# Graph network in one kernel: row splitting spread over the opening of each dense pass, halves stored in parts, counting moved off the first pieces, and identity blocks added by GpSimd

## The reference, cut to what matters

```
h = relu(layernorm(x)); x = x + L0(h)     # sum over edges with 1/sqrt(degree) weights and a self loop, times W
h = relu(layernorm(x)); x = x + L1(h)     # sum over edges plus the node itself, times W.T
h = relu(layernorm(x)); x = x + L2(h)     # mean over in-edges and over out-edges, then a GRU cell
h = relu(layernorm(x)); x = x + L3(h)     # two attention layers with batch norm
```

## Time and profile before

| what | value |
| --- | --- |
| median of three runs | 7018.52 us |
| the profiled execution | 7031.45 us, span 7029.6 us |
| PE, DVE, ACT, POOL busy | 5391.5, 5294.7, 2121.9, 3234.8 us |
| dense passes 0, 1, 2 on PE | 941.4 to 1341.8, to 1747.2, to 2157.8 us |
| turned pass on PE | 2163.7 to 2620 us |
| gather of the attention layers | 2944 indirect DMAs issued by POOL |

### The profile page before, as it was taken

One profiled execution on the slowest core, in us unless ns is written; L12 is line 12 of the kernel. 1 busy time (PEld: TensorE's weight loads), 2 busy tenths in 40 slices (PEclk: granted clock), 3 DMA queues, 4 the chain that ended last, 5 costly groups with the idle time before them and its releaser, 6 DMA issues.

```text
span 7029.6 us, 88148 instructions
## 1 busy us (share of the span) xinstructions
PE 5391.5 (77%) x33473; PEld 4175.0 (59%) x33473; DVE 5294.7 (75%) x7140; ACT 2121.9 (30%) x3520; POOL 3234.8 (46%) x3274
## 2 busy tenths in 40 slices
PE   6999979899898887377777777774377777777773
PEld 5999968788686664255555555553255555555552
DVE  7999974786783335678888888876588888888876
ACT  3555544545465443111111111112111111111111
POOL 1222100000000000777777777773777777777763
PEclk9999999999999999689888888886688988888886
DMA  4333367687789990255455455452345545545553
GB/s 148 135 123 132 123 232 256 223 266 235 267 269 221 222 189 26 56 127 127 114 128 125 116 127 123 118 127 66 74 114 128 127 114 128 127 114 128 128 127 83
DMA packets 1103488, 1021.20 MB, mean 145 GB/s; under 512 B 467063, under 2 KB 957709, under 8 KB 1098870
## 3 DMA queue, kind: packets, MB, share of 16 engines
q1 hardware_dynamic: 998150, 790.99, 39.0%
q0 software_dynamic: 104976, 225.47, 13.7%
HBM read 569.77 MB, written 346.75 MB: 130 GB/s over the span
## 4 chain that ended last, share of the span: by engine, by line
POOL 42%; issue 14%; PE 4%; DVE 3%; ACT 0%; DMA 0%; SPq 0%; POOLq 0%; DVEq 0%; ACTq 0%
POOL arena L833 39%; POOL arena L841 2%; POOL segment_terms L814 1%; PE PS L1312 1%; PE PS L1390 1%; PE PS L1403 0%; PE PS L1308 0%; PE PS L1449 0%; POOL arena L819 0%; PE PS L1291 0%; DVE arena L2150 0%; DVE arena L2151 0%; DVE arena L2247 0%; DVE arena L2246 0%; DVE arena L2238 0%
## 5 line engine op out<-in xcount | busy, mean ns | idle before, releaser
L833 POOL DMA_INDIRECT arena<-table,arena x2944 | 2794.7, 949 | 897.2 <-issue 897.2
L2046 DVE TENSOR_TENSOR arena<-shift,PS 128x1664 bf16<-128x1664 bf16 (+1 forms) x768 | 1319.7, 1779 | 3.3
L1180 PE MATMUL PS<-count_pieces,node_halves 128*128 128x512 f32 (+1 forms) x4704 | 1085.8, 388 | 70.8 <-DVE count_pieces L1783 36.6
L1036 ACT ACTIVATE arena<-PS 128x396 f32<-128x396 f32 (+1 forms) x1078 | 525.2, 490 | 1949.5 <-PE PS L1390 1943.5
L1403 PE MATMUL PS<-X,arena 128*128 128x396 bf16 x5952 | 1037.8, 331 | 0.0
L1180 PEld LDWEIGHTS PS<-count_pieces,node_halves 128*128 128x128 f32 x4704 | 858.5, 189 | 242.2 <-issue 37.2
L1390 PE MATMUL PS<-arena 128*128 128x132 f32 x6272 | 964.2, 321 | 2.6 <-DVE arena L2032 2.6
L1390 PEld LDWEIGHTS PS<-arena 128*128 128x128 f32 x6272 | 928.3, 229 | 46.1 <-issue 2.8
L1368 PE MATMUL PS<-ident,arena 128*32 128x128 f32 x392 | 101.5, 413 | 1004.1 <-DMA arena<-table,arena 1004.1
L1119 PE MATMUL PS<-arena 128*128 128x49 bf16 x7936 | 804.1, 278 | 24.5 <-DVE arena L1621 22.5
L1403 PEld LDWEIGHTS PS<-X,arena 128*128 128x128 bf16 x5952 | 570.1, 97 | 418.5 <-issue 3.6
(11 more groups left out here) (373 smaller groups left out, 4986.6 us busy)
## 6 DMA issues: line engine op xcount, KB each, us to landing
arena<-counts SPq DMA_DIRECT2D x315, 896.0 KB, 4.8
segment_sums<-arena SPq DMA_DIRECT2D x96, 2176.0 KB, 10.7
counts<-arena SPq DMA_DIRECT2D x31, 3136.0 KB, 9.4
arena<-table,arena POOLq DMA_INDIRECT x2944
vec<-edge_rows SPq DMA_DIRECT2D x192, 64.0 KB
arena<-counts SPq DMA_DIRECT2D x21, 448.0 KB, 3.4
table<-arena SPq DMA_DIRECT2D x2, 3332.0 KB, 14.1
arena<-table SPq DMA_DIRECT2D x2, 3332.0 KB, 15.0
```

Of the source, the lines that this page charges most:

```text
L833: g_.indirect_dma_start(out=ring[n % RING][:, i, :], out_offset=None, in_=table_d[j][:, :], in_offset=bass.IndirectOffsetOnAxis(ap=other[: ...
L1036: c_.activation(out_rows[:, g:g + width, 0:SW], PS[:, 4 + m % 2, 0:width * SW].rearrange("p (t f) -> p t f", f=SW), ACT.Copy)\
L1180: last = t_.matmul(PS[:, 2 + g % 2, 0:w].rearrange("p (u r) -> p u r", r=CK), X2[:, blk, t, :], PC[:, n % 3, 0:units(g), b, :], start=(blk ...
L2046: last = v_.tensor_tensor(spots[t][:, lo:hi, :], block_at[:, t, :].unsqueeze(1).broadcast_to([P, hi - lo, P]), PS[:, 3, P + lo:P + hi].uns ...
```

## The change

ACT centres the rows of pass 0 while the counts are still built (`centred_rows`), so that at the opening of pass 0 DVE only divides and takes the remainder. In all three passes the splitting is no longer done in one go: `divide`, `high` and `low` of a group stand between the first pieces' widenings, and in passes 1 and 2 the first groups are split behind the last pieces of the pass before. The index tables of pass 0 move from pieces 1 to 16 to pieces 7 to 23. DVE takes four of the seven blocks of the half-size pieces, which ACT did alone. The first three pieces of passes 1 and 2 are counted by ACT, and of the later groups DVE counts every second piece in pass 1 and ACT the others in pass 2. SP stores `node_halves` in seven parts behind pieces 14, 26, ..., 86, and issues the first three transposed loads of the turned pass as the last three pieces are widened. POOL adds the identity to the widened counts (`add_own`, 49 additions of 128x128 in each of passes 0 and 1), and PE's identity matmuls go; a piece with such a block waits for the semaphore `own_added`. To have a semaphore for that, PE's score turning in the attention layers waits for `logits` of the batch before, which its own earlier instruction has already waited for.

```diff
+        ALONE = 3
         def by_vector(n):
-            k, m = n // SLOTS, n % SLOTS
-            return (SLOTS - NPB) * k + min(m + 1, SLOTS - NPB)
+            return n + 1
+        def counted(k, g, p, by):
+            if units(g) < 2:
+                return k == 2
+            if by == "vector":
+                return k == 1 and (p >= AHEAD if g == 0 else g < SHARE or p % 2 == 0) or k == 2 and (g > 0 or p >= AHEAD)
+            return k > 0 and g == 0 and p < AHEAD or k == 2 and g >= SHARE and p % 2 == 1
+        AHEAD = 3
...
# SP
-                    if k == 2 and m == 2:
-                        sp.wait_ge(s["parts_ready"], 3 * NMG)
-                        sp.dma_start(x2_d.rearrange("(b p) f -> p b f", p=P), X2[:, :, :, :].bitcast(f32).rearrange("p b t f -> p b (t f)"))\
-                          .then_inc(s["x2_stored"], 16)
-            sp.wait_ge(s["conv_a"], 3 * SLOTS)
-            sp.wait_ge(s["conv_v"], by_vector(3 * SLOTS - 1))
-            sp.wait_ge(s["stair_sums"], 3 * STAIR)
+                    for i in range(NMG):
+                        if k == 2 and m == 14 + 12 * i:
+                            sp.wait_ge(s["parts_ready"], 2 * NMG + i + 1)
...
+                if m < 3:
+                    sp.wait_ge(s["conv_a"], 3 * SLOTS - 2 + m)
+                    sp.wait_ge(s["conv_v"], by_vector(3 * SLOTS - 3 + m))
...
# POOL
+            def add_own(k, m):
+                n, g = piece(k, m), m // NPB
+                pool.wait_ge(s["conv_a"], n + 1)
+                pool.wait_ge(s["conv_v"], by_vector(n))
+                for j in OWN[m]:
+                    part = PC[:, n % 3, (j - 4 * g) // 2, (j - OT) % PB, j % 2 * P:(j % 2 + 1) * P]
+                    g_.tensor_tensor(part, part.bitcast(f32), ident[:, :], ALU.add).then_inc(s["own_added"], 1)
...
# ACT, while the counts are built
+                        c_.activation(centred_rows[:, j - 1, :], X[:, j - 1, :], ACT.Identity, bias=stat[:, 1, j - 1:j])\
+                          .then_inc(s["row_stats"], 1)
# ACT, last pieces of a pass
+                        if m >= SLOTS - 4:
+                            high(k + 1, m - (SLOTS - 4))
                 if k < 2:
-                    for m in range(3):
-                        conv(k + 1, m)
-                    act.wait_ge(s["piece_used"], SLOTS * (k + 1))
...
+                    conv(k + 1, 0)
+                    high(k + 1, 4)
+                    conv(k + 1, 1)
+                    high(k + 1, 5)
+                    conv(k + 1, 2)
...
# PE
+                if own and OWN[m]:
+                    pe.wait_ge(s["own_added"], own_through(n))
...
-                if p == 0 and own:
-                    lo, hi = nodes_of(g)
-                    for j in range(lo, hi):
-                        for t in range(HALF):
-                            t_.matmul(PS[:, 2 + g % 2, (j - 4 * g) * P:(j - 4 * g + 1) * P], X2[:, j - OT, t, :], identr[:, :],
-                                      start=False, stop=False)
```

More of the change, by code:

```diff
@@ L356, in piece, with widened, columns @@
             return SLOTS * k + m
+        ALONE = 3
         def by_vector(n):
-            k, m = n // SLOTS, n % SLOTS
-            return (SLOTS - NPB) * k + min(m + 1, SLOTS - NPB)
+            return n + 1
         def act_half(k, g):
-            return 1 if k == 1 and g < SHARE else 0
-        def counted_by(k, g):
-            return ("vector" if (k == 1 and g < SHARE) or k == 2 else None, "scalar" if k == 2 and g >= SHARE else None)
+            return 1 if k == 1 and units(g) == 2 else 0
+        def widened(g, by):
+            if units(g) == 2:
+                return 0, PB
+            return (0, ALONE) if by == "scalar" else (ALONE, PB)
+        def counted(k, g, p, by):
[5 more added lines that the diff above has]
+        AHEAD = 3
+        BY_SCALAR = [(k, g) for k in range(3) for g in range(GR) if any(counted(k, g, p, "scalar") for p in range(NPB))]
+        def columns(v, k, g, by):
+            by_piece = v.rearrange("p (a b) -> p a b", b=PB)
+            if units(g) < 2:
+                lo, hi = widened(g, by)
+                return by_piece[:, :, lo:hi]
+            taken = [p for p in range(NPB) if counted(k, g, p, by)]
+            step = taken[1] - taken[0]
+            return by_piece[:, taken[0]:taken[-1] + 1:step, :]
         def hot_slot(t):
@@ L389, in nodes_of, with own_through @@
             return lo, min(4 * g + 2 * units(g), RT)
+        OWN = [[j for j in range(OT, RT) if j // 4 == m // NPB and (j - OT) // PB == m % NPB] for m in range(SLOTS)]
+        def own_through(n):
+            k, m = n // SLOTS, n % SLOTS
+            return NB * k + sum(len(tiles) for tiles in OWN[0:m + 1])
         LOADS = [(v, c, s_) for v in range(2) for c in CO for s_ in range(2)]
@@ L794, in _, with clear_sums @@
                   .then_inc(s[f"rows_in{j % 4}"], 16)
-            for k in range(3):
+            def clear_sums(k):
                 pool.wait_ge(s["parts_ready"], NMG * (k + 1))
@@ L890, in conv @@
                 u = act_half(k, g)
+                lo, hi = widened(g, "scalar")
                 act.wait_ge(s[f"piece_in{n % 3}"], 16 * (n // 3 + 1))
                 need(act, "piece_used", n - 2)
-                if counted_by(k, g)[1]:
-                    if p == 0:
-                        need(act, "src_counted", g - SHARE - 1)
-                    for b in range(PB):
+                if counted(k, g, p, "scalar"):
+                    nth = BY_SCALAR.index((k, g))
+                    need(act, "src_counted", nth if nth <= 2 else nth - 1)
+                    for b in range(lo, hi):
                         last = c_.activation(PC[:, n % 3, u, b, :], land[n % 3][:, u, b, :], ACT.Copy,
@@ L899, in conv @@
                 else:
-                    last = c_.activation(PC[:, n % 3, u, :, :], land[n % 3][:, u, :, :], ACT.Copy)
+                    last = c_.activation(PC[:, n % 3, u, lo:hi, :], land[n % 3][:, u, lo:hi, :], ACT.Copy)
                 last.then_inc(s["conv_a"], 1)
@@ L924, in _ @@
                 for m in range(SLOTS):
+                    if k == 0 and 3 <= m < NMG:
+                        high(0, m)
                     if m >= 3:
@@ L1702, in norm_parts @@
                 link(v_.tensor_tensor(stat[:, 2, :], stat[:, 2, :], scale, ALU.mult))
[L1703 to L1709 removed]
             def tables_behind(t):
[L1713 removed]
+                if t == -2:
                     link(v_.tensor_scalar(valid[:, 0, :], deg[:, :], 1.0, None, ALU.min))
@@ L1739, in tables_behind @@
                     link(v_.tensor_tensor(place, same, by_place, ALU.mult))
+                if t == 0:
+                    flat = [v.rearrange("p q e -> p (q e)") for v in (place, same)]
                     link(v_.tensor_tensor(place, by_place, place, ALU.subtract))
@@ L1785, in conv @@
                 else:
-                    last = v_.tensor_copy(PC[:, n % 3, u, :, :], land[n % 3][:, u, :, :])
+                    last = v_.tensor_copy(PC[:, n % 3, u, lo:hi, :], land[n % 3][:, u, lo:hi, :])
                 last.then_inc(s["conv_v"], 1)
-                if counted_by(k, g)[0] and p == NPB - 1:
+                if p == NPB - 1 and any(counted(k, g, x, "vector") for x in range(NPB)):
                     dve.wait_ge(s["conv_v"], by_vector(n))
-                    link(v_.tensor_tensor(cnt_out[:, :], cnt_out[:, :], cnt[:, g % 2, 0:NB], ALU.add))
+                    total = columns(cnt_out[:, :], k, g, "vector")
+                    link(v_.tensor_tensor(total, total, columns(cnt[:, g % 2, 0:NB], k, g, "vector"), ALU.add))
             def take_group(k, g):
```

128 lines of the change are left out of this document (72 added, 56 removed).

## The result

The changed kernel takes 6948.18 us, the median of six runs (6945.57 to 6956.06), against 7017.08 us of the kernel before in the same session: a ratio of 0.9903 (0.9893 to 0.9914), so 69 us less (60 to 75). The prediction was 6935.5, 12.7 us lower than measured and inside its range of 6913 to 6970. A second session gave 0.9903 again (0.9887 to 0.992, experiment 9).

The account below looks back on a forecast made before the run. Inside dense passes PE alone was taken to decide, at the passages DVE's program; 20.6 + 15 + 9.5 + 33 + 3 + 5 - 2 - 1 = 83 us off 7018.5 (7031.45 less 12.9) gave 6935.5, range 6913 to 6970.

Parts of the forecast that it names:

- Identity: 20.6 us: Passes 0 and 1: 196 identity matmuls of 0.105 us leave PE, POOL's additions of 0.45 us stay hidden; 20.6 us gained.
- The rival of the lock-step: Group pieces wait for four POOL additions each, shut out by DVE's widenings; at 2.6 us an addition 7076 us; chance 0.05.
- At the two pass ends with two additions each, I charge 1 us each.: Ends of passes 0 and 1, where DVE has no idle time: POOL's additions cost 1 us each, -2 in the sum.
- Opening of pass 0: 15 us: Start of pass 0: earlier first piece and no table wait, less DVE's divisions, lows and tables; 15 us gained (9 to 21).
- 9.0 + 1.5 - 2 - 5.5 = 3: Pass 0 behind its first piece: table wait 9.0 and late pieces 1.5 gained, splitting 2 and table stall 5.5 given back.
- Passage 0 to 1: 9.5: Piece 105 to the next pass's fourth piece: DVE's shorter list gains 8 us, the higher clock 1.5; 9.5 (3 to 18.4).
- 1 to 2: 33: Passage from pass 1 to 2: 66.0 us becomes 34.5, the store's wait goes, clock 1.5; 33 us gained (26 to 39.5).
- End of pass 2: 3: Half pieces ending pass 2: three blocks on ACT and four on DVE end PE's 0.87 us waits; 3 us (0 to 4).
- turned pass: 5: Turned pass: first transposed load goes out two half pieces earlier, and this carries through to the end; 5 us (2 to 7).
- late pass 1: -1: Late pieces of pass 1: DVE counts four of seven, busy 38 of 50 us, fits but bunched; 1 us lost.
- The store's parts: Rival in pass 2: seven store parts delay the loads behind them by 4 us of PE each, 28 us; 6963; chance 0.08.
- The openings: Rival: DVE's extra round trips and late tables and lows stall PE; openings bring only 5, 2 and 24; 6968; chance 0.13.

Follow-up runs that it names:

- experiment 9: The changed kernel run again without an edit, in another session: 6951.02 us, 0.9903 of the kernel before.
- experiment 2: The changed kernel with the identity multiplied by TensorE again and no additions on POOL: 6963.7 us, 0.9909 of the kernel before.
- experiment 4: The changed kernel with each identity block added, subtracted and added again on POOL: 7035.31 us, 1.0012 of the kernel before.
- experiment 12: The changed kernel with only the last group's identity at the ends of passes 0 and 1 on TensorE again: 6949.15 us, 0.9895 of before.
- experiment 11: The changed kernel with both pass-end edits (last group's identity on TensorE, ACT's square later), pass 0's divisions earlier and tables in ten steps: 6934.98 us, 0.9884.
- experiment 3: The changed kernel with the halves stored whole in one 6.3 MB DMA behind piece 2 of pass 2: 6985.03 us, 0.9937 of before.
- experiment 6: The changed kernel with the splitting at the two passages in the old order, all lows behind the last group: 6952.26 us, 0.992 of before.
- experiment 5: The changed kernel with the first three pieces of passes 1 and 2 counted by DVE again instead of ACT: 6944.77 us, 0.9905 of before.

## Why the prediction was right, and where it was off

**Identity: 20.6 us.** Right in the price: pieces 28 to 105 are 9.8 and 8.8 us shorter, an addition is 0.46 us where 0.45 was taken, and its cover is 1.1 us a block on average, as worked out. Of the 20.6 us, 7 to 14 are left at the turned pass (experiment 2): the rest goes at the pass ends and, where nothing was charged for it, at the opening of pass 0. The rival of the lock-step is a real mechanism: it was to turn the whole change around at 2.0 us a block, and at 1.66 us (163.0 us of POOL for 98 blocks in experiment 4) it has, because slower pieces follow the waits. One addition of 0.46 us stays far from it.

**"At the two pass ends with two additions each, I charge 1 us each."** This term was mis-sized. In passes 0 and 1 the last two blocks fall on the last half piece, where DVE works without a pause, PE has nothing queued, and the layer's last product waits behind. Taking them off (experiment 12) shortens the passages by 1.5 and 3.2 us against one profile of after, 4.2 and 3.5 against the other: 4.7 to 7.7 in all instead of 2. The prediction priced the additions by their own length. What they cost is two locked additions, 2.43 us, and in executions like that of experiment 9 also the last piece and the product behind it at the lower clock. Without them the passages gain 9.8 to 10.1 and 33.1 to 33.6 us, so the 9.5 and 33 below were right but for this term.

**Opening of pass 0: 15 us.** Measured 10.3 to 12.7 at piece 28, of which the identity matmuls that are gone make 0.6 (six at 0.105). The 12.1 us of the first piece is exact. The step that failed is "9.0 + 1.5 - 2 - 5.5 = 3" for what follows: it came to nothing (from 2.1 lost to 1.1 gained over the pairs of profiles). PE's gaps there are 8.6 us in one profile and 10.4 in the other, against 9.0 before. I had the list late by 4 us (3.81), but set 28 us of table steps and widenings against 22 us of PE as one sum over seven pieces. The table steps stand in two heaps, and three buffers don't bridge a heap of two steps (1.89 + 1.89 us and 1.89 + 3.63 us) around two widenings; 2.49 us of the gaps are the wait for POOL's first additions. Experiment 11, which spreads the tables, fills DVE's wait for the first load and moves POOL's clearing behind, gets 8.5 to 10.7 us.

**Passage 0 to 1: 9.5, and 1 to 2: 33.** Measured 5.6 to 8.6 and 29.6 to 30.4. DVE's list was right (32.7 worked out, 32.2 busy), and so was the store (a wait of 25.3 us taken, 24.1 to 24.4 in experiment 3); what is short is the pass-end term above, which lies inside these stretches. Experiment 6 shows that the order is worth 11 to 14 us of the sum; how much of the rest is ACT's counting stays open (experiment 5).

**End of pass 2: 3, turned pass: 5, late pass 1: -1.** Measured: 4.4 at the end of pass 2, and 1.0 lost late in pass 1 (pieces 28 to 105: 268.8 us against 267.7 in pass 0). The turned pass starts 3.5 to 4.2 us closer to the last piece; that its end moves as much is not shown.

**The sum.** At the first matmul of the turned pass the gain is 72.5 to 80.9 us over the pairs of profiles, on average 76.7; 83 was predicted. The timed medians differ by 69 (60 to 75). So some 6 of the 14 us missing are the opening and the pass ends. The other 8 lie between the marks and the medians. The profiles that make up the average come from several sessions and chips, the turned pass alone varies by 25 us over all runs, and 76.7 is just outside the interval of the timed gain: whether anything behind the dense passes became slower stays open. The subtraction of 12.9 us for the long profile was sound: its repeat is 10.8 us shorter.

**The rivals.** The store's parts don't come back: no PE gap lies behind them, no load of pass 2 lands more than 8.8 us after its issue in either profile (22.8 before), and the whole store costs 24.4 us where it stood, 14 to 15 even behind piece 14. The openings gave back some of what was expected of them, but 6 to 12 us of 57.5 instead of the 26.5 that the rival had.

## What to carry to other kernels

Work moved to an idle engine is cheap by its sum and dear by its worst place: look at the last piece of a stage, where nothing is queued behind it, and price it there with the engine that it locks out, and is locked out by, at full work. Where a helper's work must fit beside a pipeline with a few buffers, count it piece by piece and not per stretch: the same table work left PE gaps of 8.6 us in two heaps and 1.8 us in ten steps, with other work moved out of the way. A wait on TensorE can cost more than its length: behind some waits of 2 to 3.5 us a piece ran at the lower clock, behind others not. The next rows of the timeline tell, and also whether anything waited for the slow piece.

## What was not expected of the hardware

The first three additions took 1.16 to 1.29 us each, beside a DVE that was catching up, where most take 0.46 at a pitch of 0.42. A widening on DVE beside POOL's clearing (5.48 us) took over 6 us of its own: two widenings 7.24 us.

```profile
1021.83 5.48 POOL L839 MEMSET arena<- 128x6400 f32 x1 [8.32 <-DMA group_resets<-arena]
...
1022.00 7.24 DVE L1845 CAST count_pieces<-arena 128x1792 fp32r<-128x1792 bf16 x2 [2.12 <-PE PS L1249]
```

And the clock decides between repeats of one kernel (experiment 9): with the last piece at the same distance from the two ahead of it, the same passage was 2.7 us longer where the lower clock fell on that piece and the product behind it instead of on the two ahead.
